# Reciprocals of eight columns and a widening copy in place of a reciprocal written 512 columns wide

## What is computed

```
def _dense_branch(X, wqkv, wo):
    qkv = einsum('bth,hnd->bntd', X, wqkv);  Q, K, V = split(qkv, 3)
    Q, K = _rope(Q, pos), _rope(K, pos)
    att = einsum('bnqd,bnkd->bnqk', Q, K) / sqrt(64)
    att = where(tril(ones((t, t))), att, -inf)
    AV = einsum('bnqk,bnkd->bnqd', softmax(att), V)
    return concat_heads(AV) @ wo
x = x + tanh(g_ffn[3]) * (_mosa_branch(h) + _dense_branch(h))
```

## Time and profile before

| | |
|---|---|
| median of 3 runs | 536.26 us (535.94 to 537.78) |
| the profiled execution | 535.96 us |
| its span | 533.8 us |
| busy: TensorE, VectorE, ScalarE, GpSimd | 461.0, 301.3, 231.7, 94.7 us |
| last layer's feed-forward part, about 373 us to the end: TensorE, VectorE | 134.7, 108.2 us of 161 |
| mean granted TensorE clock, as a share of full speed | 0.958 |

### The profile page before, as it was taken

The page is one execution under the profiler, slowest core; times in us unless marked ns, Lnnn a source line. Parts: engine busy times, 40 slices in busy tenths (PEclk is TensorE's granted clock), DMA queues, the critical chain, the costliest instruction groups (busy, mean ns, idle before and its releaser), DMA issues.

```text
span 533.8 us, 6952 instructions
## 1 busy us (share of the span) xinstructions
PE 461.0 (86%) x2690; PEld 260.8 (49%) x2690; DVE 301.3 (56%) x559; ACT 231.7 (43%) x447; POOL 94.7 (18%) x87
## 2 busy tenths in 40 slices
PE   5889999989898985888789988898868979899876
PEld 2334433644763332777337744333444556465543
DVE  1667765434235445864255645465986487675871
ACT  4345563310322655453343354456715445554441
POOL 3000000230501003441000000024550505135000
PEclk9899999889999998999799999999958989999989
DMA  8500000710000000000000020010110001101000
GB/s 355 218 2 1 2 1 0 261 42 0 1 0 2 0 0 1 0 2 1 0 2 0 1 79 1 0 22 0 22 20 14 7 3 19 20 2 21 21 0 21
DMA packets 4595, 15.54 MB, mean 29 GB/s; under 512 B 1362, under 2 KB 1619, under 8 KB 4051
## 3 DMA queue, kind: packets, MB, share of 16 engines
q1 hardware_dynamic: 4562, 15.10, 8.6%
HBM read 12.73 MB, written 0.52 MB: 25 GB/s over the span
## 4 chain that ended last, share of the span: by engine, by line
PE 61%; DVE 23%; ACT 9%; issue 5%; POOL 1%; DMA 1%; SPq 0%; DVEq 0%; POOLq 0%
PE PS L502 54%; DVE sw L2307 4%; DVE mxd L2284 2%; PE PS L1200 2%; PE PS L735 2%; ACT xc L1406 1%; DVE mx L1845 1%; DVE wmoe L1838 1%; ACT xc L1407 1%; DVE keys L1992 1%; POOL wmoe L2508 1%; PE PS L573 1%; DMA cst<-const_dram 1%; DVE yb L2321 1%; DVE hp L1796 1%
## 5 line engine op out<-in xcount | busy, mean ns | idle before, releaser
L502 PE MATMUL PS<-PTB,keys 128*64 128x128 f32 (+4 forms) x416 | 46.5, 404 | 0.1
L1710 ACT COPY PTB<-PS 128x768 f32<-128x768 f32 (+1 forms) x24 | 20.9, 870 | 46.0 <-PE PS L1200 45.7
L1992 DVE TENSOR_REDUCE keys<-PS 128x9 f32<-128x693 f32 x32 | 26.6, 874 | 10.8 <-PE PS L502 10.8
L2526 POOL TENSOR_TENSOR den<-den,cst 128x1024 f32<-128x1024 f32 x7 | 16.9, 2421 | 87.3 <-DMA den<-wmoe 87.3
L502 PE MATMUL PS<-keys,PTB 32*128 32x231 f32 (+2 forms) x384 | 29.6, 349 | 3.0 <-DVE keys L1967 1.6
L502 PEld LDWEIGHTS PS<-PTB,keys 128*64 128x64 f32 (+3 forms) x416 | 22.8, 150 | 18.7 <-issue 14.1
L502 PE MATMUL PS<-x,cst 128*128 128x512 f32 x32 | 19.5, 710 | 13.4 <-DMA cst<-const_dram 5.8
L2508 POOL TENSOR_TENSOR wmoe<-wmoe,mx 128x616 f32<-128x616 f32 x16 | 19.5, 1216 | 63.1 <-DVE mx L1847 63.1
L502 PEld LDWEIGHTS PS<-keys,PTB 32*128 32x128 f32 (+1 forms) x384 | 21.2, 190 | 17.7 <-issue 12.8
L1796 DVE TENSOR_TENSOR hp<-PS,xc 128x512 f32<-128x512 f32 x16 | 11.1, 691 | 30.6 <-ACT xc L1407 30.6
L502 PE MATMUL PS<-wmoe 64*128 64x512 f32 (+3 forms) x128 | 24.6, 482 | 4.1 <-ACT mask L1698 3.0
(11 more groups left out here) (345 smaller groups left out, 1000.5 us busy)
## 6 DMA issues: line engine op xcount, KB each, us to landing
wmoe<-w_dram SPq DMA_DIRECT2D x2, 2048.0 KB, 11.8
den<-wmoe SPq DMA_DIRECT2D x28, 64.0 KB, 2.3
wa<-wa_dram SPq DMA_DIRECT2D x4, 256.0 KB, 6.6
wlate<-ew_dram SPq DMA_DIRECT2D x2, 512.0 KB, 5.7
wd<-wd_dram SPq DMA_DIRECT2D x1, 1024.0 KB, 9.8
wlate<-wm_dram SPq DMA_DIRECT2D x1, 1024.0 KB, 4.8
cst<-const_dram SPq DMA_DIRECT2D x1, 738.0 KB, 7.9
cst<-const_dram SPq DMA_DIRECT2D x1, 670.5 KB, 4.6
```

The lines of the kernel that those rows point to most:

```text
L502: return nc.tensor.matmul(o, l, r, start=start, stop=stop, skip_group_check=True)
L1710: nc.scalar.copy(PTR[n % 2][:, :, 0:width], PS[:, 4:6, 0:width]).then_inc(S("d_turned"), 1)
L1992: last = v.tensor_reduce(mxn[:, 2 * half + t, :].rearrange("p (g r) -> p g r", r=32)[:, :, 12:15], PS[:, 0:NG, t * 256:t * 256 + GK].rearr ...
L2526: g.tensor_tensor(turned, turned, table("ropes"), ALU.mult).then_inc(S("d_roped"), 1)
```

## The change

`recip(r)` takes the reciprocals of the eight sums once, into a new small tile `recd` (128 x 8), waits for its own result by `link`, and then writes `wide` by a copy that reads each of the eight columns 64 times. The waits ahead of it and the increment behind it are as they were, the latter now on the copy.

```diff
         mxd = sb("mxd", [128, 2, 2, 2])

+        recd = sb("recd", [128, TB, 2])
         wide = sw13[:].rearrange("p a t -> p (a t)")
...
                     if r > 0:
                         dve.wait_ge(S("d_spread"), r)
-                    v.reciprocal(wide.rearrange("p (t z f) -> p t z f", t=TB, z=2),
-                                 dend[:, r % 2].unsqueeze(3).to_broadcast([128, TB, 2, 64])).then_inc(S("d_shares"), 1)
+                    link(v.reciprocal(recd[:], dend[:, r % 2]))
+                    v.tensor_copy(wide.rearrange("p (t z f) -> p t z f", t=TB, z=2),
+                                  recd[:].unsqueeze(3).to_broadcast([128, TB, 2, 64])).then_inc(S("d_shares"), 1)
```

## The result

The changed kernel takes 517.04 us (median of 4 runs, 516.82 to 518.73); the kernel before, in 4 runs, 536.57 us. The ratio is 0.964, with a 95% interval of 0.9613 to 0.9667. The forecast was 524.5 us with a range of 520.7 to 529.3. The sign was right; the gain is 19.5 us where 12 were forecast.

What follows compares the result with a forecast made beforehand. The chain of waits was 61% TensorE, 23% VectorE, the wide reciprocal 4%. Savings of 10.1 us at the reciprocals plus 1.5 us of clock, 11.6 from 535.96, gave 524.4, stated as 524.5 us; range 520.7 to 529.3.

Steps and rivals of the forecast that it cites:

- r = 0: First reciprocal: TensorE waits 3.59 us for the selection's end, then 1.80 us for column sums, moving whole; saves 2.62 us.
- The price of one `recip`: On VectorE, a small reciprocal (0.24 us) plus copy (0.40 us) costs 0.64 us in place of 3.26, saving 2.62.
- r = 1, 3, 4, 5, 6: Second, fourth, fifth, sixth and seventh reciprocals, TensorE waiting behind each: save 1.86, 0.92, 0.68, 1.40 and 2.62 us.
- Rival 1: Indirect places (fourth to sixth reciprocals) hand nothing on, clock still falls after the seventh: 7.1 us stay, 528.9 us; 15%.
- r = 2: Third reciprocal: the next mask addition already waited 0.40 us for TensorE, whose work covers it; saves 0.
- The clock behind r = 6: TensorE's fall to 1.2 GHz after the seventh reciprocal's 3.41 us idleness vanishes; saves 1.5 us.
- The clock around r = 0: TensorE's half-speed stretch from 386-387 to 403-404 us: between -3.7 and +1.3 us, taken as 0.
- rival 2: The slow stretch around the first reciprocal ends early or never begins, giving 3.7 us more: 520.7 us; 13%.
- The clock at 434 us: TensorE's half-speed stretch at 434 to 438 us, ahead of the third spread; the prediction had no term for it.

## Why the prediction was wrong

The steps that failed are three terms of the sum: r = 0, held to be a wait that moves as a whole, and the clock in two places, put at nothing. Together they are 5.4 of the 5.6 us by which the traces missed it.

- **The price of one `recip`: right.** 0.19 + 0.43 us; the next instruction starts 384.24 - 383.62 = 0.62 us behind the first, where 0.64 was reckoned, 2.64 saved where 2.62 was. The lower bound for the copy, L2364's 0.484, was still too high. The Trainium skill's rule in VectorE: DVE Perf Modes, "The perf-mode tier table", is agreed with by this trace: the copy between SBUF tiles takes 0.432 us and L1885's out of PSUM 0.692.
- **r = 0: the step that failed first.** "The first wait is longer than the saving, and the second moves as a whole." The second did not move, it went: it held 3.2 us of VectorE standing for GpSimd, and the place gave 4.42 us, not 2.62. The row that says so was in my hands, three additions of 128 x 16 in 3.79 us where a 128 x 64 one took 0.21, and I took the sum as a fixed duration.
- **r = 1, 3, 4, 5, 6: right**, each within 0.11 us, by comparing what VectorE gains with when the scores are ready and how long TensorE waits. Rival 1 did not occur.
- **r = 2: 0 was right for the sum, and wrong as a statement on the reciprocal.** In the kernel before the half-speed stretch at 434 us covered it. In the changed kernel that cover is gone, and a wide third reciprocal costs 7.4 us there, 6.3 of them by the meeting with GpSimd. The step named the cover and did not ask what becomes of it.
- **The clock behind r = 6: right**, 1.68 us where 1.5 was reckoned. The fall follows that wait in three traces of four, so it is a matter of odds and not certain.
- **The clock around r = 0: taken as 0, between -3.7 and +1.3; 2.1 us were gained.** The fall came, as forecast, at the same moment; but the return came 10 us sooner, at 393 to 394 us. That is rival 2, half of it. How much of this the change caused is open. All seven traces with a small first reciprocal and no filling have the eight transposes 15.3 to 16.1 us behind it; of the three traces with a wide one and nothing moved on GpSimd, two have 22.2 and 21.8 and one 20.4. So about 1.8 of the 2.1 us can be luck, the traced execution of the kernel before being a slow one at this place.
- **The clock at 434 us: missed altogether**, 1.6 us. It was in the trace, and I listed only stretches next to a reciprocal that binds. A half-speed stretch stands ahead of the third spread in four of the five traces whose second reciprocal is wide, and in none of the eight in which it is small; so the change is what takes it away, most likely, but by which way is not shown. TensorE's waits ahead of it, 0.81, 0.43 and 1.43 us, stand in the changed kernel as they were (0.81, 0.43 and 1.44), so they alone don't explain it.
- **The range** held the clock's uncertainty once. It had no room for a gain from an engine that is not on the path, and none for luck at three stretches of clock.
- **2.3 us of the 19.5** lie between the profiled executions and the other runs of the two kernels, 1.7 of them on the changed kernel's side. No trace shows them; this stays open.

The meeting is told in the Trainium skill as well, in SBUF — State Buffer, section "SBUF: two separate sides": VectorE and GpSimd have a pair of ports in common, taken as an exclusive lock for a whole instruction by whichever starts first, by VectorE only in its two-port modes or, against a GpSimd instruction that reads SBUF, with two SBUF inputs. This case's traces agree: 2.48 and 2.83 us in place of 0.68 for such instructions, 0.67 as ever for the one with an input in PSUM, and 2.80 in place of 2.36 us for GpSimd's product where the mask had started first.

## What to carry to other kernels

Before a duration goes into a sum, compare it with rows of the same kind and size: an instruction several times too long is a wait in disguise, and moving it can remove the wait or make one. When an engine off the critical path works in bursts whose start hangs on something else (here GpSimd behind a transfer), ask of every shift which instructions it moves into or out of a burst; the price of one place can then hang on what was done at another (nothing for the third reciprocal in the kernel before, 7.4 us in the changed one). Don't read a sum of places from one trace of each kernel: here the traces gave 0 and 11.2 us apart and 17.2 together, and the run times 6 and 13 against 19. And the clock comes and goes from one execution to the next at the same place with the same waits, so look for half-speed stretches also where the change touches nothing, and give each a range and not a value.

## What was not expected of the hardware

- VectorE's additions and GpSimd's products of 128 x 1024 exclude one another for whole instructions: a 0.17 us addition took 2.27 us, until GpSimd's instruction ended.
- A small difference in arrival decides: 2.6 us later on VectorE turned a step of 0.59 us into one of 3.8, and a wide reciprocal of 3.3 us that nothing waited for into a loss of 7.4.
- A reciprocal costs 6.2 to 6.3 ns for each further column (0.192 us for 8 columns, 3.34 for 512), and 3.34 us for 512 whichever way it reads; a copy of 512 columns that reads each of eight 64 times costs 0.43 us, as a contiguous one does.
